# Coupled split projections: two products at a time, their terms alternating between two PSUM banks

## The reference, cut to what matters

```python
q = jnp.einsum('bti,oi->bto', x, Wq).reshape(Bx, Tx, H, D).transpose(0, 2, 1, 3)
k = jnp.einsum('bti,oi->bto', x, Wk).reshape(Bx, Tx, H, D).transpose(0, 2, 1, 3)
v = jnp.einsum('bti,oi->bto', x, Wv).reshape(Bx, Tx, H, V).transpose(0, 2, 1, 3)
g = jnp.einsum('bti,oi->bto', x, Wg)
...
scores = jnp.einsum('bhtd,bhsd->bhts', q, k) * D ** (-0.5)
scores = scores * decay[None]
o = jnp.einsum('bhts,bhsv->bhtv', scores, v)
...
o = o * jax.nn.silu(g)
return jnp.einsum('btc,oc->bto', o, Wo)
```

## Time and profile before

| | |
|---|---|
| median of 3 runs | 769.07 us |
| span of the profiled execution, first to last instruction | 764.9 us |
| around that span, up to the median | 4.2 us |
| PE busy | 736.1 us, 96% of the span |
| DVE busy | 623.1 us, 81% |
| POOL busy | 587.1 us, 77% |
| ACT busy | 452.3 us, 59% |

### The profile page before, as it was taken

One profiled execution on the slowest core, in us unless ns is written; L12 is line 12 of the kernel. 1 busy time (PEld: TensorE's weight loads), 2 busy tenths in 40 slices (PEclk: granted clock), 3 DMA queues, 4 the chain that ended last, 5 costly groups with the idle time before them and its releaser, 6 DMA issues.

```text
span 764.9 us, 29122 instructions
## 1 busy us (share of the span) xinstructions
PE 736.1 (96%) x12121; PEld 648.9 (85%) x12121; DVE 623.1 (81%) x1326; ACT 452.3 (59%) x819; POOL 587.1 (77%) x641
## 2 busy tenths in 40 slices
PE   5788999999999999999999999999999999999996
PEld 4566888898988988889898889889888888988875
DVE  6988787988879887888979888797888888787545
ACT  4244546666575566656556565655656565656664
POOL 2757777887878888797878977788887978777651
PEclk9899999999999999999999999999999999999998
DMA  9422221122123122222312212231321222122100
GB/s 326 126 43 44 44 43 39 29 43 53 29 44 71 32 62 43 44 51 43 72 27 67 43 40 56 43 70 24 71 43 36 60 43 55 25 59 43 38 15 28
DMA packets 65235, 41.41 MB, mean 54 GB/s; under 512 B 38096, under 2 KB 54736, under 8 KB 65104
## 3 DMA queue, kind: packets, MB, share of 16 engines
q1 hardware_dynamic: 64384, 38.75, 21.8%
q10 hardware_dynamic: 720, 0.80, 0.3%
HBM read 10.17 MB, written 4.19 MB: 19 GB/s over the span
## 4 chain that ended last, share of the span: by engine, by line
PE 91%; DVE 4%; issue 1%; ACT 1%; DMA 1%; POOL 1%; SPq 0%; ACTq 0%; DVEq 0%; POOLq 0%
PE ring L275 51%; PE outs L275 14%; PE O_E L275 14%; PE ring L290 7%; PE O_O L275 3%; PE ring L314 2%; DMA consts<-in_const 1%; DVE N L922 1%; DVE swapped L871 1%; POOL gn_rstd L1150 0%; DVE turned L866 0%; DVE gn_sum L915 0%; POOL y L1157 0%; DVE h_full L851 0%; DMA k_odd<-rot_k 0%
## 5 line engine op out<-in xcount | busy, mean ns | idle before, releaser
L1157 POOL TENSOR_TENSOR y<-y,gate 128x512 f32<-128x512 f32 x123 | 155.1, 1284 | 27.3 <-ACT y L628 27.3
L1140 POOL TENSOR_TENSOR rot_k<-rot_k,sin_k 128x256 f32<-128x256 f32 x128 | 108.6, 870 | 35.5 <-DVE sin_k L888 35.5
L275 PEld LDWEIGHTS outs<-wo_gated,y 128*128 128x128 f32 x992 | 127.2, 191 | 9.6 <-POOL y L1157 1.7
L275 PE MATMUL outs<-wo_gated,y 128*128 128x128 f32 x992 | 131.3, 275 | 1.1 <-POOL y L1157 1.0
L915 DVE TENSOR_REDUCE gn_sum<-N 128x4 f32<-128x512 f32 x128 | 81.8, 680 | 42.4 <-ACT N L616 42.4
L1150 POOL TENSOR_TENSOR gn_rstd<-gn_var,minus_half 128x8 f32<-128x8 f32 x64 | 105.4, 1646 | 5.0
L1134 POOL TENSOR_TENSOR qT<-qT,swapped 128x512 f32<-128x512 f32 x64 | 83.1, 1299 | 19.6 <-DVE swapped L871 19.4
L628 ACT ACTIVATE y<-ring,gn 128x512 f32<-128x512 f32 x126 | 90.9, 777 | 4.8 <-PE ring L290 4.8
L597 ACT ACTIVATE v_odd<-ring 128x512 f32<-128x512 f32 x64 | 38.3, 599 | 93.0 <-PE ring L275 93.0
L895 DVE TENSOR_TENSOR A<-ring,consts 128x256 f32<-128x256 f32 x128 | 47.9, 416 | 40.0 <-PE ring L275 40.0
L909 DVE TENSOR_TENSOR S<-ring,S 128x512 f32<-128x512 f32 x112 | 76.8, 686 | 1.9
(11 more groups left out here) (150 smaller groups left out, 2122.9 us busy)
## 6 DMA issues: line engine op xcount, KB each, us to landing
v<-v_odd SPq DMA_DIRECT2D x128, 128.0 KB, 2.3
k_odd<-rot_k SPq DMA_DIRECT2D x128, 64.0 KB, 2.2
X<-in_x SPq DMA_DIRECT2D x16, 256.0 KB, 3.3
out<-X SPq DMA_DIRECT2D x15, 256.0 KB, 3.1
key_tables<-in_const SPq DMA_DIRECT2D x7, 256.0 KB, 8.2
rotary_q<-in_const_q SPq DMA_DIRECT2D x2, 512.0 KB, 8.7
N<-in_w_qkT SPq DMA_DIRECT2D x1, 512.0 KB, 5.0
N<-in_w_vT SPq DMA_DIRECT2D x1, 512.0 KB, 6.2
```

The costliest lines, as they stand in the source:

```text
L275: return e.matmul(o, lhsT, rhs, start=start, stop=stop, skip_group_check=True)
L1140: done = e.tensor_tensor(turned[:, n, :, :], turned[:, n, :, :], sin[:, n, :, :], op)
L1157: e.tensor_tensor(y[:, n % NY, :], y[:, n % NY, :], gate[:, n % 2, :], ALU.mult).then_inc(sem["y"])
```

## The change

`split_matmuls` takes two products and issues their terms in turn: first term of the one, first of the other, and so on. The functions that projected now only take their bank, state their waits and return the operands; three new functions couple them. Queries of one chunk go with the odd values of another (61 couples; at the edges of the loop each goes alone), the two gates of a chunk together (64 couples), the even values with the next keys (63 couples). Both banks of a couple are taken, with both sets of waits, ahead of its first matmul. `project_ffn_out`, which stood between queries and odd values, now stands ahead of the couple. No other engine's program is changed.

```diff
+            def split_matmuls(*products):
+
+                for l, r in ((0, 0), (0, 1), (1, 0)):
+                    done = [matmul(o, lhsT[l], rhs[r], l + r == 0, l == 1) for o, lhsT, rhs in products]
+                return done
...
+            def project_q_v(m, i):
+
+                if i < 0:
+                    split_matmul(*query_product(m)).then_inc(sem["proj_q"])
+                elif m >= NCHUNK:
+                    split_matmul(*value_product(i, 1)).then_inc(sem["proj_v_O"])
+                else:
+                    q, v_odds = split_matmuls(query_product(m), value_product(i, 1))
+                    q.then_inc(sem["proj_q"])
+                    v_odds.then_inc(sem["proj_v_O"])
+
+            def project_v_k(i):
+
+                if i < 0:
+                    split_matmul(*key_product(i + 1)).then_inc(sem["proj_k"])
+                elif i + 1 >= NCHUNK:
+                    split_matmul(*value_product(i, 0)).then_inc(sem["proj_v_E"])
+                else:
+                    v_evens, k = split_matmuls(value_product(i, 0), key_product(i + 1))
+                    v_evens.then_inc(sem["proj_v_E"])
+                    k.then_inc(sem["proj_k"])
...
-                split_matmul(bank[:, :], [wg[s][:, cols] for s in ("hi", "lo")], h_parts(g)).then_inc(sem["gate_psum"])
+                return bank[:, :], [wg[s][:, cols] for s in ("hi", "lo")], h_parts(g)
+
+            def project_gates(i):
+
+                even, odd = split_matmuls(gate_product(2 * i), gate_product(2 * i + 1))
+                even.then_inc(sem["gate_psum"])
+                odd.then_inc(sem["gate_psum"])
...
-                for m in due(step + 4, 1, NCHUNK):
-                    project_q(m)
                 for g in due(step - 13, GC, LAST - 1):
                     project_ffn_out(g)
-                for i in due(step + 1, 1, NCHUNK):
-                    project_v(i, 1)
+                for m in due(step + 4, 1, NCHUNK + 3):
+                    project_q_v(m, m - 3)
                 for i in due(step - 4, 1, NCHUNK):
-                    project_gate(2 * i)
-                for i in due(step - 4, 1, NCHUNK):
-                    project_gate(2 * i + 1)
+                    project_gates(i)
...
-                for i in due(step + 1, 1, NCHUNK):
-                    project_v(i, 0)
-                for i in due(step + 2, 1, NCHUNK):
-                    project_k(i)
+                for i in due(step + 2, 1, NCHUNK + 1):
+                    project_v_k(i - 1)
```

More of the change, by code:

```diff
@@ L315, in transpose_n, with query_product @@
                 done.then_inc(sem[f"n{which}T"])
-            def project_q(m):
+            def query_product(m):
                 g, p = divmod(m, PAIRS)
@@ L323, in project_q, with key_product @@
                 at.wait_ge("hT_lo", g + 1)
-                split_matmul(bank[:, :], [wqk[s][:, cols] for s in ("hi", "lo")], h_parts(g)).then_inc(sem["proj_q"])
-            def project_k(i):
+                return bank[:, :], [wqk[s][:, cols] for s in ("hi", "lo")], h_parts(g)
+            def key_product(i):
                 g, j = divmod(i, GC)
@@ L331, in project_k, with value_product @@
                 at.wait_ge("hT_lo", g + 1)
-                split_matmul(bank[:, :], h_parts(g, slice(j * P, (j + 1) * P)), [wqk[s][:, H * D:2 * H * D] for s in ("hi", "lo")]
-                             ).then_inc(sem["proj_k"])
-            def project_v(i, odd):
+                return bank[:, :], h_parts(g, slice(j * P, (j + 1) * P)), [wqk[s][:, H * D:2 * H * D] for s in ("hi", "lo")]
+            def value_product(i, odd):
                 g, j = divmod(i, GC)
@@ L341, in project_v @@
                 at.wait_ge("hT_lo", g + 1)
-                split_matmul(bank[:, :], h_parts(g, slice(j * P, (j + 1) * P)), [wv[s][:, cols] for s in ("hi", "lo")]
-                             ).then_inc(sem["proj_v_" + "EO"[odd]])
+                return bank[:, :], h_parts(g, slice(j * P, (j + 1) * P)), [wv[s][:, cols] for s in ("hi", "lo")]
+            def project_q_v(m, i):
[16 more added lines that the diff above has]
+                    k.then_inc(sem["proj_k"])
             def transpose_k(i):
@@ L408, in recall, with gate_product @@
                 done.then_inc(sem["o"])
-            def project_gate(n):
+            def gate_product(n):
                 g, h = divmod(n, H)
```

## The result

The changed kernel takes 788.07 us, median of 4 runs (786.52 to 789.53), against 768.99 for the kernel before, measured beside it (767.07 to 770.2). The ratio is 1.0256, 95% interval 1.0233 to 1.0279: slower by 2.6%, some 19.7 us. 789.5 had been forecast. The span of the profiled execution grew from 764.9 to 786.2 us, where 785.3 was the sum.

A forecast was written before the change was run, and what follows sets the result against it. PE's own stream was taken to bound the kernel. Gates 15.5, FFN steps 4.4 and start 0.5 us, on 764.9 us, gave 785.3; with 4.2 us around the span 789.5 us, range 778 to 802.

The forecast's parts named there:

- the sum: Profiled execution's 764.9 us plus 15.5 (gates), 4.4 (FFN steps) and 0.5 (start), 20.4 us in all, giving 785.3 us.
- What bounds: Whole kernel: the time is the length of PE's own stream, PE being busy 96% of the span.
- Alternating, taken as 0: Split products on PE: alternating banks costs nothing; bounds from no cost to 22.6 us over 1128 matmuls.
- the rival in which the bank pays: Coupled matmuls: alternating saves up to 0.020 us each, 22.6 us, giving 766.9 us; half gives 778; 6 in 100.
- The gates, 15.5 us: Ordinary steps: 37 gate couples wait for `S` ahead of the even gate, 0.42 us each; bounds 9.6 to 19.2 us.
- The rival in which the waits are cheaper: Gate couples: additions end earlier or response and restart overlap matmuls, 11 us in all, 780 us; 16 in 100.
- FFN steps, 4.4 us: 12 FFN steps: queries start 0.10 us late, even values wait 0.27 us for `product`, 0.37 us a step.
- The rival in which this carries into the next step: FFN steps: DVE's 0.88 us lateness reaches the next step's masks and norms, 10.6 us more, 800 us; 8 in 100.
- The other couples, 0: Ordinary steps: queries with odd values, and even values with keys, lose nothing to their moved waits.
- the start: Kernel's start: the first queries of a couple wait for the low value weights, with a restart some 0.5 us.
- The term of 4.2 us around the span: Time outside the profiled span: 4.2 us added to 785.3 us to reach the forecast 789.5 us.

## Why the prediction was right

**What bounds.** PE's own stream, with no idle time inside a step. It held: the 15.3 us that the gate couples lose in the trace came out in full at the end, 16.0 us for the gates' couple alone.

**Alternating, taken as 0.** It held. The distances are 0.23 us before and after; the mean of those under 0.3 us between two matmuls of split projections is 232.9 ns before and 231.8 ns with all three couples alternating, so 0.001 us a matmul at most. Three kernels that alternate with the waits covered show no gain: two couples at 1.0021, the gates' couple at 1.0064 against 1.0082 for its base, all three at 1.0064, which is what the waits left over in it had been put at. Over its own base of 1.0026 the last is 2.9 us, less than those waits (4.5 us) by no more than the intervals allow. With this the rival in which the bank pays, 0.010 to 0.020 us a matmul, is out. The Trainium skill's distance of 215.8 ns ("TensorE: Matmul & The Clock Gate", "Back-to-back issue gap") is not reached by alternating; the trace has 0.23 us in every order tried.

**The gates, 15.5 us.** Measured by the gates' couple alone: 16.0 us; in the trace 0.43 us in most of the waiting steps, where 0.42 was worked out, and 0.53 in a few. That it is 35 steps and not 37 makes up for these. The response, forecast at 0.06 us and measured at 0.05 in all but a few, and the restart of 0.10 were taken from one place at 69 us and held. The rival in which the waits are cheaper (9.6 us) fell with this.

**FFN steps, 4.4 us.** Taking the product back saved some 5.4 us, and the step grew by 0.39 us where 0.37 was forecast. DVE took the queries up 0.87 us late, forecast 0.88. The rival in which this carries into the next step fell: step 34 grew by the gates' price alone.

**The other couples, 0.** Right for the change as it stands, and for the reason given: the gates' delay covers the wait for `cos_q`. Without that cover the wait is real, 0.12 us at 16 places in the kernel with the gates apart. That was said only as a possibility and with no price.

**The count of the sum.** The 1.4 us between forecast and median are two errors that partly cancel. The span of the changed kernel came out 0.9 us over its sum of 785.3. Half a microsecond of that is the start, which was mis-sized: PE's wait for `sin_k` there grew to 3.3 us from 1.0, while that of 1.6 us for L868 (now L894) shrank to 0.3, about 1 us more where 0.5 was in the sum. The term of 4.2 us around the span was too large. Time and span of one and the same execution are 1.9 us apart (788.08 and 786.2 us for the profiled one of the changed kernel, and 1.8 to 2.0 in nearly all the others). The other 2.3 us of the 4.2 are there because the profiled execution of before was quicker than its median, which is also why the span grew by 21.3 us and the median by 19.1. The forecast is closer than its terms by this luck.

The step that failed was one of the experiments, not of the forecast: the output head as a cover. Its reasoning looked at what the moved work waits for in the middle of the kernel, and neither at its waits at the end nor at who waits for what it delays.

## What to carry to other kernels

When resources are taken for two operations at once, the wait of the second moves ahead of the first. Read in the trace of before by how much each buffer is free ahead of time, and subtract the time by which the wait moves: a margin of 0.44 us against a wait that moved by 0.70 us was most of the result, 16 of 19.7 us. Test such a wait by moving its release on the other engine while the waiting engine's program stays as it is; and before work is moved to cover a wait, look up who waits for what it pushes back, in the last steps of the loop as well as in the middle.

## What the runs showed of the hardware that was not expected

The response of PE to a release depends on how its waits are written. Where the couple waits for one semaphore (`S`), PE starts 0.05 us after DVE's end: 410.95 to 411.00 above. Where it waits for `cos_q` and then for `S`, which has long been there, it is 0.14 us: 429.35 to 429.49. In the kernel with the gates apart this is so at all 16 places of the kind, 0.146 us or a little more. The number of waits alone does not do it. In the FFN steps of the changed kernel the even values wait for `cos_q` and then for `product`; here the first one comes 1.2 us earlier (in step 33 `cos_q` at 401.27, `product` at 402.50) and the last one is awaited, and the response is 0.05 us in all 12. So a short wait can cost 0.1 us more because a second, long satisfied one stands behind it in PE's program. No run exchanged the two waits of one place, so this order as the cause is read from the traces and not tested.
